# Cross-attention with 16-wide heads: scores by 64-row tiles of one head each, joint maxima, one turn per half batch, one P-times-V visit per four heads

## The reference, cut to what matters

```python
# B=16, S=256 queries, D=320, C=512, 256 keys (248 text, 4 "dummy", 4 "ip"), 20 heads of 16
q = split_heads(x @ w_q)
out_text = softmax(q @ k.T / 4) @ v                  # k, v from the 248 text keys
mask_ip  = 0 or -10000, per query and special key, from bbox and a 16x16 grid
out_ip   = softmax(q @ k_ip.T / 4 + mask_ip) @ v_ip  # 8 special keys, weights w_k_ip, w_v_ip
out = merge_heads(out_text + out_ip) @ w_out + b_out + x
```

## Time and profile before

| | |
|---|---|
| median of three runs | 576.11 us |
| lowest and highest | 575.31, 578.98 us |
| span of the profiled execution, first to last instruction | 572.9 us |
| PE busy | 546.0 us (95%) |
| DVE busy | 431.8 us (75%) |
| ACT, POOL busy | 300.7, 139.9 us |
| mean granted clock of TensorE | 0.989 of full |
| DMA | 110.75 MB in 89591 packets, mean 193 GB/s |

### The profile page before, as it was taken

How to read it: one execution, slowest core, us unless ns; L and a number is a source line. 1 busy time by engine, 2 the same in 40 slices (tenths; PEclk the granted TensorE clock), 3 DMA queues, 4 the chain that set the end, 5 groups by cost and what they waited for, 6 DMA issues and landing times.

```text
span 572.9 us, 13438 instructions
## 1 busy us (share of the span) xinstructions
PE 546.0 (95%) x3984; PEld 364.1 (64%) x3984; DVE 431.8 (75%) x1122; ACT 300.7 (52%) x517; POOL 139.9 (24%) x206
## 2 busy tenths in 40 slices
PE   3999899999999799999999999999999999999995
PEld 2788688788787455666656566556565665566552
DVE  2767342532536789999999999999999999999822
ACT  3642443534442556566665665655656665656660
POOL 9241000000000312323323323323233233232241
PEclk9999999999999989999999999999999999999996
DMA  8988888888989887775865876769658767677101
GB/s 268 371 239 179 266 293 294 275 295 253 297 269 267 235 222 149 171 178 118 211 156 122 209 131 177 177 136 203 165 110 217 127 159 192 137 189 177 31 23 46
DMA packets 89591, 110.75 MB, mean 193 GB/s; under 512 B 9568, under 2 KB 68576, under 8 KB 89568
## 3 DMA queue, kind: packets, MB, share of 16 engines
q1 hardware_dynamic: 88928, 109.19, 71.1%
q0 software_dynamic: 640, 1.28, 1.4%
HBM read 72.22 MB, written 38.21 MB: 193 GB/s over the span
## 4 chain that ended last, share of the span: by engine, by line
PE 81%; DVE 6%; DMA 4%; issue 3%; SPq 3%; ACT 1%; POOL 1%; POOLq 0%; DVEq 0%; ACTq 0%
PE pv L900 19%; PE score_t L884 17%; PE score_q L827 12%; PE pj L913 9%; PE score_t L786 2%; PE score_t L787 2%; PE score_t L788 2%; PE pj L786 2%; PE pj L787 2%; DMA k_stack<-k_parts 2%; PE pj L788 2%; PE pv L788 2%; PE pv L786 2%; PE pv L787 2%; PE score_q L786 1%
## 5 line engine op out<-in xcount | busy, mean ns | idle before, releaser
L596 ACT ACTIVATE probs<-score_t 128x512 f32<-128x512 f32 x320 | 182.8, 598 | 143.3 <-PE score_t L884 143.2
L675 DVE TENSOR_REDUCE max_cols<-score_q 128x2 fp32r<-128x496 f32 x320 | 208.3, 653 | 15.0 <-PE score_q L827 11.7
L884 PE MATMUL score_t<-q_stack,k_stack 128*128 128x256 f32 x640 | 160.6, 334 | 0.5 <-ACT probs L596 0.5
L884 PEld LDWEIGHTS score_t<-q_stack,k_stack 128*128 128x128 f32 x640 | 107.1, 190 | 84.2 <-ACT probs L596 50.0
L900 PE MATMUL pv<-probs,v_cur 128*32 128x256 f32 x1920 | 136.6, 387 | 0.7 <-ACT o_all L585 0.6
L827 PE MATMUL score_q<-k_stack,q_stack 128*128 128x512 f32 x320 | 126.6, 400 | 6.6 <-DMA k_stack<-k_parts 3.9
L488 POOL TENSOR_TENSOR o_turned<-o_turned,inv_cols 128x256 f32<-128x256 f32 x80 | 49.8, 622 | 185.6 <-DVE inv_cols L741 185.6
L900 PEld LDWEIGHTS pv<-probs,v_cur 128*32 128x32 f32 x1920 | 46.2, 108 | 53.4 <-issue 27.4
L913 PE MATMUL pj<-wo_sb,o_all 128*128 128x320 f32 x192 | 64.7, 447 | 2.9 <-DVE o_all L748 2.3
L827 PEld LDWEIGHTS score_q<-k_stack,q_stack 128*128 128x128 f32 x320 | 60.6, 190 | 9.6 <-DMA k_stack<-k_parts 5.0
L738 DVE STREAM_TRANSPOSE o_turned<-o_all 128x512 f32<-128x512 f32 x80 | 55.0, 688 | 9.0 <-ACT o_all L585 7.9
(11 more groups left out here) (134 smaller groups left out, 673.4 us busy)
## 6 DMA issues: line engine op xcount, KB each, us to landing
q_stack<-q_parts SPq DMA_DIRECT2D x96, 160.0 KB, 3.0
k_stack<-k_parts SPq DMA_DIRECT2D x192, 80.0 KB, 3.4
v_rows<-v_out SPq DMA_DIRECT2D x32, 320.0 KB, 2.5
v_cur<-v_rows SPq DMA_DIRECT2D x16, 640.0 KB
o_all<-in_ctxT SPq DMA_DIRECT2D x16, 512.0 KB, 5.7
q_parts<-qk_out SPq DMA_DIRECT2D x32, 256.0 KB, 2.4
k_parts<-qk_out SPq DMA_DIRECT2D x32, 248.0 KB, 4.3
q_stack<-aux_rows SPq DMA_DIRECT2D x32, 160.0 KB, 3.5
```

The source lines that it names most:

```text
L596: nc.scalar.activation(probs[:, slot(u, p), 2 * S * e:2 * S * (e + 1)], score_t[:, 512 * e:512 * e + 512], ACT.Exp, scale=SCALE)\
L675: nc.vector.tensor_reduce(out=max_cols[:, h, t, at:at + 2], in_=both[:, :, 0:TEXT], op=ALU.max, axis=AX.X, negate=True)
L884: last = mm(score_t[:, 512 * e + S * t:512 * e + S * t + S], k_cols(u, p, e, t, P), q_cols(u, p, 0, S), start=True, stop=True)
```

## The change

- **Stacks.** Each head of a pair gets 64 partitions of its own: head 0 from partition 0, head 1 from partition 64. There they hold q high, low, high (48 rows, `PART`), five mask rows (`MASKS`) and two rows for the maxima. `k_stack` has only 256 columns a pair, with no zero blocks. The mask and one-row constants are loaded once by DMA. POOL's fills and ACT's copies of constants go.
- **Query scores**: four matmuls a pair (t by e) of 53 contraction rows and 256 columns; head e goes to its own bank, both t side by side. They wait and signal once a pair.
- **Key scores**: four matmuls a pair of 55 rows and 256 columns, tile by tile with the heads alternating. They wait once a pair, for both exponentials of the pair before.
- **Maxima**: two reductions a pair, over the two banks of both heads at once, instead of four.
- **Turn**: one transpose of 128x64 a half batch instead of four of 32x64. The rows now lie on 128 partitions, so their store is four DMAs with runs of 32 elements, and the load of rows is two DMAs.
- **Loads**: the q stack of a half batch is eight DMAs instead of four (six of 16 rows by five pairs, two of the five mask rows); k stays at six.
- **P times V**: all three kinds in one visit, in pairs 2, 4, 6, 8 and 0 of the next batch, between the pair's key scores and query scores. `EVACUATE` and `INVERT` come one pair earlier.
- In the first stage the split context has its own tensor `c_hl`, and the first query scores use two banks, one pair at a time.

```diff
-        k_stack = sb("k_stack", [P, 2, PAIRS * 2 * KEYS], f32r)
+        k_stack = sb("k_stack", [P, 2, PAIRS * KEYS], f32r)
+        def q_cols(par, p, e, rows, a, n):
+            return q_stack[HEAD * e:HEAD * e + rows, par, p * S + a:p * S + a + n]
...
             def store_rows(b, h):
                 sp.wait_ge(rows_turned, 2 * b + h + 1)
-                sp.dma_start(max_rows[h], row_buf[0:4 * HALF, h, :]).then_inc(rows_stored, 16)
+                for i in range(4):
+                    sp.dma_start(max_rows[h].rearrange("r (t i n) -> i r t n", t=2, i=4)[i],
+                                 row_buf[32 * i:32 * i + 32, h, :].rearrange("r (t n) -> r t n", t=2))\
+                        .then_inc(rows_stored, 16)
...
-                for quad, part in enumerate((0, 1, 0)):
-                    src = q_parts[part, 32 * ps:32 * (ps + n), bass.ds(b * S, S)].rearrange(
-                        "(a r) n -> r a n", r=32)
-                    sp.dma_start(qv[32 * quad:32 * quad + 32, :, :], src).then_inc(done, 16)
-                src = aux_rows[bass.ds(b, 1), :, :].rearrange("a r n -> (a r) n")
-                sp.dma_start(qv[96:128, :, :], src.unsqueeze(1).broadcast_to([32, n, S])).then_inc(done, 16)
+                for e in range(2):
+                    for j, part in enumerate((0, 1, 0)):
+                        src = q_parts[part, 32 * ps:32 * (ps + n), bass.ds(b * S, S)].rearrange(
+                            "(a e r) n -> e r a n", e=2, r=DH)[e]
+                        at = HEAD * e + DH * j
+                        sp.dma_start(qv[at:at + DH, :, :], src).then_inc(done, 16)
+                    src = aux_rows[bass.ds(b, 1), :, :].rearrange("a r n -> (a r) n")
+                    at = HEAD * e + PART
+                    sp.dma_start(qv[at:at + MASKS, :, :], src.unsqueeze(1).broadcast_to([MASKS, n, S]))\
+                        .then_inc(done, 16)
...
+            def maxima(b, p):
+                both = score_pair(isinstance(b, int) and b == 0, p)
+                nc.vector.tensor_reduce(out=max_cols[:, h, :, at:at + 2].rearrange("p t e -> p e t"),
+                                        in_=both[:, :, :, 0:TEXT], op=ALU.max, axis=AX.X, negate=True)
...
+                nc.vector.transpose(row_buf[:, h, :].rearrange("p (t n) -> p t n", t=2),
+                                    max_cols[:, h, :, :].bitcast(f32)).then_inc(rows_turned, 1)
...
+            def query_scores(b, u, p):
+                    need(pe, max_done, n if first else n - 1)
+                for t in range(2):
+                    for e in range(2):
+                        last = mm(score_bank(first, p, e)[:, t * KEYS:(t + 1) * KEYS],
+                                  q_cols(u, p, e, PART + MASKS, t * P, P),
+                                  k_cols(u, p, e, PART + MASKS, 0, KEYS), start=True, stop=True)
+                last.then_inc(sq_ready, 1)
...
+            def key_scores(b, u, p):
+                need(pe, exp_done, 2 * (PAIRS * b + p))
+                for tile in range(2):
+                    for e in range(2):
+                        last = mm(score_t[:, 512 * e + S * tile:512 * e + S * tile + S],
+                                  k_cols(u, p, e, PART + MASKS + 2, tile * P, P),
+                                  q_cols(u, p, e, PART + MASKS + 2, 0, S), start=True, stop=True)
+                        if tile:
+                            last.then_inc(st_ready, 1)
...
-VALUES = {p: [((p - 2) // 2, (0, 1) if p % 2 == 0 else (2,), 0)] for p in range(2, PAIRS)}
-VALUES[0], VALUES[1] = [(QUADS - 1, (0, 1), -1)], [(QUADS - 1, (2,), -1)]
-EVACUATE = {3: [(0, 0)], 5: [(1, 0)], 7: [(2, 0)], 9: [(3, 0)], 1: [(4, -1)]}
-INVERT = {4: [(0, 0)], 6: [(1, 0)], 8: [(2, 0)], 0: [(3, -1)], 2: [(4, -1)]}
+VALUES = {p: [((p - 2) // 2, 0)] for p in range(2, PAIRS, 2)}
+VALUES[0] = [(QUADS - 1, -1)]
+EVACUATE = {2: [(0, 0)], 4: [(1, 0)], 6: [(2, 0)], 8: [(3, 0)], 0: [(4, -1)]}
+INVERT = {3: [(0, 0)], 5: [(1, 0)], 7: [(2, 0)], 9: [(3, 0)], 1: [(4, -1)]}
```

More of the change, by code:

```diff
@@ L26 @@
 VW = 2 * D
-AUX = 9
+PART = 3 * DH
+HEAD = 64
+MASKS = 1 + NIP
 HALF = PAIRS // 2
@@ L558, in group @@
                     qk_tile(g, j)
-                    if last and j < 5:
-                        act.wait_ge(stacks_set, j - 2)
-                        cols = slice((j - 3) * HALF * 2 * KEYS, (j - 2) * HALF * 2 * KEYS)
-                        nc.scalar.activation(
-                            k_stack[96:128, 1, cols].rearrange("p (a n) -> p a n", a=HALF),
-                            kaux_raw.unsqueeze(1).broadcast_to([32, HALF, 2 * KEYS]), ACT.Copy)\
-                            .then_inc(stacks_set, 1)
                 if first:
@@ L680, in turn @@
-            def turn(b, h):
-                dve.wait_ge(max_done, 2 * (PAIRS * b + HALF * (h + 1)))
-                need(dve, rows_stored, 16 * (2 * b + h - 1))
-                to = row_buf[:, h, :].rearrange("r (t i n) -> r t i n", t=2, i=4)
-                for i in range(4):
-                    last = nc.vector.transpose(to[:, :, i, :], max_cols[32 * i:32 * i + 32, h, :, :].bitcast(f32))
-                last.then_inc(rows_turned, 1)
+                dve.wait_ge(sq_ready, PAIRS * b + p + 1)
@@ L689, in first_maxima @@
+            def turn(b, h):
+                dve.wait_ge(max_done, PAIRS * b + HALF * (h + 1))
+                need(dve, rows_stored, 64 * (2 * b + h - 1))
+                nc.vector.transpose(row_buf[:, h, :].rearrange("p (t n) -> p t n", t=2),
+                                    max_cols[:, h, :, :].bitcast(f32)).then_inc(rows_turned, 1)
             def first_maxima(tile):
                 for p in FIRST_SCORES.get(tile, ()):
-                    for t in range(2):
-                        maxima(0, p, t)
+                    maxima(0, p)
@@ L760, in batch @@
                 for p in range(PAIRS):
-                    for t in range(2):
-                        if there(b, 1) and there(b):
-                            maxima(b + 1, p, t)
-                        if t == 0:
-                            for c, off in TURN_BACK.get(p, ()):
-                                if there(b, off):
-                                    turn_back(b + off, (u + off) % 2, c)
-                            for k, off in INVERT.get(p, ()):
-                                if there(b, off):
-                                    invert(b + off, k)
-                            for m, off in FINISH.get(p, ()):
-                                if there(b, off):
-                                    finish(b + off, (u + off) % 2, m)
+                    if there(b, 1) and there(b):
+                        maxima(b + 1, p)
+                    for c, off in TURN_BACK.get(p, ()):
+                        if there(b, off):
+                            turn_back(b + off, (u + off) % 2, c)
+                    for k, off in INVERT.get(p, ()):
+                        if there(b, off):
+                            invert(b + off, k)
+                    for m, off in FINISH.get(p, ()):
+                        if there(b, off):
+                            finish(b + off, (u + off) % 2, m)
                     if p % HALF == HALF - 1 and there(b, 1) and there(b):
@@ L851, in group @@
                         for p in FIRST_SCORES.get(n, ()):
-                            for t in range(2):
-                                query_scores(0, 0, p, t)
+                            query_scores(0, 0, p)
                 if first:
@@ L973 @@
     gy, gx = _np.meshgrid(line, line, indexing="ij")
[L975 to L979 removed]
+    kaux = _np.zeros((MASKS + 2, KEYS), f)
+    kaux[0, TEXT:TEXT + NIP] = 1
     for j in range(NIP):
[L981 removed]
+        kaux[1 + j, TEXT + NIP + j] = 1
+    kaux[MASKS, :TEXT] = 1
+    kaux[MASKS + 1, TEXT:] = 1
     vones = _np.ones((P, 1), f)
```

178 lines of the change are left out of this document (71 added, 107 removed).

## The result

The changed kernel takes 654.85 us (651.95 to 657.42, four runs) against 577.55 for the kernel before: a ratio of 1.135, 95% interval 1.130 to 1.140. The forecast was 569, its range ended at 593. Here and in the table of the experiments, times and ratios are those of the fast runs; one run of e8 and two of e10 (625.3 and 626.7 us, the former profiled) fell in a slower state and are left out.

What follows compares the result with a forecast made beforehand. TensorE, busy 546.0 of 572.9 us, was taken to bound the kernel before, SyncE's loop the changed one: 572.9 + 15 x (21.8 - 22.67) + 6 = 566, plus 3.2, so 569 us; whole range 547 to 593.

Steps and rivals of the forecast that it cites:

- the passage: Way into the batch loop: 16 more SyncE issues ahead of a late k load add 6 us; 10 would refute.
- the tail: Behind the last turn: one visit saved against one exponential wait, so a change of 0.
- The loop: Turn, SyncE's issues, k load, pair 5's query scores, VectorE's maxima, next turn: sets a period of 21.8 us.
- 11.3 to the landed k load: SyncE behind the turn: last k load issued at 8.2 us, landing 3.1 later.
- 9.9 for VectorE's second half: VectorE's work in the second half of a batch, from 10.32 us down to 9.9.
- A slack of some 3 us: Kernel before: k load lands 8.5 us behind the turn, VectorE takes up pair 5 only behind its next turn, 11.85 later.
- the new wait for two exponentials: TensorE's key scores wait for both exponentials of the pair before: 2.0 us a batch.
- Row tiles: TensorE's scores: two heads' 64-row matmuls and weight loads run side by side, 0.47 us a pair instead of 0.94.
- rival A: TensorE's row tiles or their weight loads run in turn: period up 0.53, 590 us; chance 0.18.
- One visit: TensorE's P-times-V in one visit of 24 pieces: 1.62 us instead of 1.97, 8.1 a batch instead of 9.9.
- Projections between 64-row scores: TensorE's output projections at four places a batch: mode changes cost 0.20 us each, 0.8 a batch.
- Rival C: TensorE's clock falls behind its idle time at pair 5: 1.7 us lost a batch, period 23.5, 595 us; chance 0.08.

Runs made afterwards that it cites:

- e8: Changed kernel with the old turn and one store of maxima, SyncE ordered q loads, rows store, k loads, rows load; 595.0 us, ratio 1.031.
- e10: Kernel before with only its store of maxima rows cut in four, in 128-byte runs; 617.3 us, ratio 1.069.
- e11: Changed kernel with only a pair's query scores issued ahead of the P-times-V visit; 624.4 us, ratio 1.078.
- e4: Changed kernel with 32 filler matmuls of 256 columns ahead of each of the two waits at pair 5; 635.6 us, ratio 1.099.
- e9: Changed kernel with old turn, one store, SyncE order q loads, rows store, k loads, rows load, and query scores ahead of P-times-V; 557.2 us, ratio 0.966.
- e3: Kernel before with only its q, aux and rows loads and its stores of maxima cut as the change cuts them; 679.1 us, ratio 1.174.

## Why the prediction was wrong

Of the 86 us between 569 and 654.9 the period makes 84 (27.4 and not 21.8, fifteen times) and the passage 9; the tail gives back 5. The 3.2 us added to the span were 1.3 too many: every run on record lies 1.8 to 2.0 above its own span.

**The loop was right, its price wrong.** The step that failed is "11.3 + 0.5 for the first matmuls + 9.9 of VectorE's second half = 21.7". Each term, in the period from 354.24:

- *11.3 to the landed k load*: 12.7 (366.93 is the first matmul behind it). The q, aux and rows issues were right (4.30 for 4.3); the k issues were 0.5 quicker and the landing 0.6 later than put. The four stores were priced at 1.6, with 0.35 for each further one, a price that no row showed for a store; they measure 2.75. A store of 128-byte runs from 32 partitions takes SyncE 0.63, where the store of 20 KB in whole rows takes 0.3. Those 1.15 us are most of the term's error.
- *9.9 for VectorE's second half*: 15.1, from 366.93 to the turn's end at 382.04. This is the larger error, 4.7 us with the 0.5. I took the busy time of the bound engine for a stretch in which both engines begin from nothing. TensorE had lost its lead, so both worked in turns. With TensorE's order of e11 the stretch is 11.8, so 3.3 of the 4.7 hang on that order.
- Counted by pieces, about 2.3 of the 4.7 are the low clock: 0.80, 1.36, 0.72 (three pieces) and 2.49 against the normal 0.45, 0.81, 0.43 and 1.43 of this kernel make 2.25; e4, whose filler takes time too, gets 1.4 of a period back. TensorE stands idle for 1.3 before the projection at 374.52, waiting for VectorE. The two ways of counting overlap, and how the clock and the order share the rest stays open.

**The slack was read at the wrong engine.** "A slack of some 3 us" was VectorE's. TensorE was the bound and ran 2 us ahead of it (323.78 against the turn's end near 325.8); its slack was 1.3. e10, where the chain grows by 3.0, shows that what goes beyond the 1.3 costs time.

**TensorE's order.** The forecast listed what stands behind the new wait for two exponentials, and that wait is there (20.2 us in all on TensorE's matmuls, 1.3 a batch where 2.0 were put down; no run takes it out). It didn't name what the place of the visit does: query scores 1.4 us later in even pairs, and VectorE's maxima, additions and turns back, for which projections wait, bunched behind them. e8 against e9 and the changed kernel against e11 give 38 and 30 us.

**What was right.** Row tiles: 0.24 a group, against 0.47 a pair for two groups, loads included; rival A falls. One visit: 1.43 and 0.20 for leaving it, 1.63 against 1.62. Maxima 1.07 and 0.10.

**What was small and wrong.** The tail, taken as 0, gave 5. Projections between 64-row scores were taken at 0.20 a place; four pieces now show 1.34 in the chain, where the 0.54 of two would make 1.08, and the scores behind them 0.43 and not 0.24, so some 0.45. The Trainium skill's page TensorEngine Tiling (Array Packing), section Key Properties, has a change of mode drain the engine; the trace agrees, with these numbers.

**The passage** was put at 6 and is 14.9, past the 10 that the prediction named as a sign of being wrong. e3 has 9.4 of it and e10 6.4, so the cut DMAs explain about 9. What makes the other 5 wasn't tried; the first scores with two banks and a clock of 0.81 between 180 and 220 us (0.96 before) are both there. All changed kernels carry 11 to 20 us in it, e9 too (15).

**Rival C**, the loop with the low clock on top, was named at the right place, at 0.08. Its clock term of 1.7 a batch was near (2.25 by pieces); its 595 fell short by what the loop itself had wrong. The 654.9 is the loop, the clock and the order together, and each was shown by a run that takes it away: 48 (stores), 19 net (clock), 30 (order). Together that is more than the 77 us between the two kernels: a run that shortens the stall or keeps TensorE fed also gives clock back, so the three can't be added.

## What to carry to other kernels

Ask of a longer chain what slack the bound engine has, not the one at its end. An engine that waited restarts without its lead, so the stretch behind the wait costs a serial sum and not the larger busy time (15.1 us where 9.9 were counted), and here TensorE ran it at half its clock. Where a change saves matmul time through more and smaller DMAs, order the issuing queue first: what depends on nobody ahead of what waits, and the flight of a store beside other issues.

## What the runs showed of the hardware

- SyncE issues a store of 64 runs of 128 bytes in 0.59 us, and one of 40 such runs in 0.75 to 0.84 (e10), against 0.30 for 20 runs of 1 KB; loads of 16 rows and of 32 take 0.35 and 0.33 at the median.
- Two 64-row tiles with 128 weight columns each ran side by side, in float32r, weight loads too: four matmuls of 256 columns every 0.24 us.
- Two waits of 1.6 and 2.1 us, 0.5 us of matmuls between them, were followed by about 5 us at a granted clock of 0.53, nearly all at the 1.2 GHz level; with 1.9 us of filler in front of each wait (e4) it was 0.98 on the mean of 100 us, against 0.93 and 0.90 without.
